# Twelve of sixteen expert-weight splits on GpSimd, all its down-weight work there too, and shorter lone recurrent steps in an adaLN, quantised-FFN, RNN and MoE kernel

## The reference

```python
def layer(x, cond, ...):
    # 1. per-batch modulated and normalised 128x128 weight times x   (L0_cond)
    # 2. quantised FFN; each act_qdq divides by the max |value| of a WHOLE tensor:
    x = act_qdq(x)
    up   = act_qdq(x @ lpbq_dequant(w_up).T)       # weights: one scale per 32 values
    gate = act_qdq(x @ lpbq_dequant(w_gate).T)
    gate = act_qdq(gate * fixed_qdq_u16(sigmoid(gate)))
    x1   = x_in + act_qdq(gate * up) @ lpbq_dequant(w_down).T
    # 3. recurrence over 128 times, 16 batches: h = tanh(x1_t @ Wx + b + h @ Wh)
    # 4. MoE: 8 experts of 512 hidden units, top 2 by router logits of h, softmax gates
    out  = x1 + sum_of_two(gate_e * (gelu(h @ w1_e.T + b1_e) @ w2_e.T + b2_e))
```

## Time and profile before

| what | value |
|---|---|
| runs | 293.18, 294.99, 294.94 us; median 294.94 |
| profiled execution | 293.55 us, of it span 291.8 us |
| PE / PEld busy | 259.8 / 204.2 us (89% / 70%) |
| DVE busy | 254.5 us (87%) |
| ACT busy | 213.6 us (73%) |
| POOL busy | 77.7 us (27%) |

### The profile page before, as it was taken

The page is one execution under the profiler, slowest core; times in us unless marked ns, Lnnn a source line. Parts: engine busy times, 40 slices in busy tenths (PEclk is TensorE's granted clock), DMA queues, the critical chain, the costliest instruction groups (busy, mean ns, idle before and its releaser), DMA issues.

```text
span 291.8 us, 7134 instructions
## 1 busy us (share of the span) xinstructions
PE 259.8 (89%) x2726; PEld 204.2 (70%) x2726; DVE 254.5 (87%) x629; ACT 213.6 (73%) x455; POOL 77.7 (27%) x148
## 2 busy tenths in 40 slices
PE   8999550068999999999999999999999999999994
PEld 4844240027856889888887888888778878878784
DVE  4997999999997899799887899788799987899875
ACT  5889899997832778677766766766567667688992
POOL 3368997050025412113112103111110411101000
PEclk9999955569999999999999999999999999999999
DMA  6993342103300000000000000000001000001000
GB/s 185 313 333 73 76 79 50 22 0 68 78 2 0 1 2 3 2 0 21 2 2 1 2 19 10 3 2 0 2 3 36 3 2 0 2 2 39 0 3 27
DMA packets 24039, 10.75 MB, mean 37 GB/s; under 512 B 13355, under 2 KB 22982, under 8 KB 24006
## 3 DMA queue, kind: packets, MB, share of 16 engines
q1 hardware_dynamic: 23470, 10.05, 13.9%
q10 hardware_dynamic: 536, 0.26, 0.3%
HBM read 6.11 MB, written 1.05 MB: 25 GB/s over the span
## 4 chain that ended last, share of the span: by engine, by line
PE 73%; DVE 10%; issue 1%; ACT 1%; DVEq 0%
PE bank L905 73%; DVE big L737 2%; DVE peak L645 2%; DVE big L884 1%; DVE big L749 1%; PE bank L1040 0%; DVE wyT L791 0%; DVE x_sb L771 0%; DVE big L880 0%; DVE big L756 0%; DVE big L744 0%; DVE c L764 0%; ACT wyT L465 0%; DVE wyT L839 0%; ACT big L552 0%
## 5 line engine op out<-in xcount | busy, mean ns | idle before, releaser
L905 PE MATMUL bank<-big,wt 128*128 128x384 f16 (+2 forms) x480 | 124.3, 336 | 0.5 <-DVE big L884 0.5
L905 PE MATMUL bank<-wt,big 128*128 128x128 f16 x1536 | 110.8, 219 | 0.5 <-DVE big L884 0.5
L905 PEld LDWEIGHTS bank<-wt,big 128*128 128x128 f16 x1536 | 98.2, 97 | 16.1 <-DVE big L884 0.7
L884 DVE TENSOR_TENSOR big<-big 128x384 f16<-128x384 f32 (+2 forms) x160 | 93.0, 587 | 18.1 <-ACT big L603 14.1
L601 ACT ACTIVATE big<-bank,miscT 128x384 f32<-128x384 f32 (+2 forms) x160 | 96.2, 602 | 13.6 <-PE bank L905 10.5
L905 PEld LDWEIGHTS bank<-q,wxh 128*128 128x128 f32 x254 | 44.9, 190 | 13.6 <-ACT q L564 2.0
L905 PEld LDWEIGHTS bank<-big,wt 128*128 128x128 f16 x480 | 49.6, 117 | 4.3 <-issue 0.6
L589 ACT ACTIVATE q<-bank 128x16 f32<-128x16 f32 x112 | 20.5, 183 | 38.0 <-PE bank L905 37.7
L414 POOL CAST big<-q 128x64 f16<-128x64 f32 x32 | 12.4, 388 | 125.7 <-ACT q L589 123.2
L880 DVE CAST big<-big 128x512 f16<-128x512 f32 (+2 forms) x104 | 39.0, 375 | 4.4 <-ACT big L601 4.2
L839 DVE SCALAR_TENSOR_TENSOR wyT<-bank,gates,wyT 128x128 f32<-128x128 f32 x128 | 39.8, 343 | 0.1
(11 more groups left out here) (168 smaller groups left out, 310.7 us busy)
## 6 DMA issues: line engine op xcount, KB each, us to landing
wnat<-in_w SPq DMA_DIRECT2D x8, 512.0 KB, 7.4
x_sb<-in_x SPq DMA_DIRECT2D x4, 256.0 KB, 4.4
out_block<-wyT SPq DMA_DIRECT2D x15, 64.0 KB
wn<-in_w_gate ACTq DMA_DIRECT2D x1, 192.0 KB, 4.8
wn<-in_w_up SPq DMA_DIRECT2D x1, 192.0 KB, 5.8
wn<-in_w_down SPq DMA_DIRECT2D x1, 192.0 KB, 5.8
b_in<-in_b SPq DMA_DIRECT2D x12, 4.0 KB
wt<-wyT SPq DMA_TRANSPOSE x8, 3.0
```

The costliest lines, as they stand in the source:

```text
L884: V.tensor_tensor(g_lo[:, par, f, 0:w], g32[:, f, 0:w], g_hi[:, par, f, 0:w], ALU.subtract).then_inc(g_lo_done, 1)
L905: return nc.tensor.matmul(o, l, r, start=start, stop=stop, skip_group_check=True)
```

## The change

- `W_POOL` goes from 8 to 12: chunks 8 to 11 are split on GpSimd, and SP transposes both parts. The buffer still has eight places (`NATS`), so GpSimd first waits for the eight earlier transposes. Four chunks are left to ScalarE and TensorE, and ScalarE's wait in front of them is now for twelve DMAs. `spread_peak(4)` stands before the last of them.
- `scale_weights(2)` goes ahead of the splits; the two parts of the down weights are made on GpSimd, behind chunk 11 and the parts of b2, from an fp32 copy that ScalarE takes out of PSUM (`wd32`, `wd_done`). The block scales of up and down are made in one set, in the front.
- `split_weights(0, 1)` goes ahead of `scale_weights(1)`.
- VectorE: `weight_lo(1)` one peak later; the first quarter of gate x sigmoid goes into the trip of peak 2; nothing is left in the trips of peaks 3 and 4.
- ScalarE: the two g2 quantisations go ahead of the Gelu table and of the four copies of x.
- The first 256 columns of the recurrence's input use one fp32 matmul on `x1` in place of three on its parts, so `split_x1(0)` goes; the first steps start half-way through chunk 1 in place of ahead of chunk 2. The transposes of x1 stand between the lone steps, the fourth group in the MoE's slot 1.
- The router's two parts are one operand of 16 columns; VectorE adds the halves as it copies them.
- The last expert's three tiles have a bank each, so each can be added when its own matmuls are done.
- `WARM_Q` goes from 8 to 2.

```diff
-W_POOL = 8
+W_POOL = 12
...
-WARM_START, WARM_COND, WARM_C, WARM_Q = 5, 2, 4, 8
+WARM_START, WARM_COND, WARM_C, WARM_Q = 5, 2, 4, 2
...
             scale_weights(0)
+            pool.wait_ge(c_mm, NK)
+            split_weights(0, 1)
             scale_weights(1)
...
-            pool.wait_ge(c_mm, NK)
-            split_weights(0, EARLY_SPLITS)
+            scale_weights(2)
+            split_weights(1, EARLY_SPLITS)
...
-            split_weights(EARLY_SPLITS, W_POOL)
-            scale_weights(2)
+            split_weights(EARLY_SPLITS, NATS)
+            split_b2()
+            pool.wait_ge(wt_t[0], 16 * NATS)
+            split_weights(NATS, W_POOL)
+
+            pool.wait_ge(wd_done, 1)
+            G.tensor_copy(wT_hi[:, 2 * NJ:NW, :], wd32[:, :, :]).then_inc(wT_hi_done, 1)
+            pool.wait_ge(wT_hi_done, 3)
+            G.tensor_tensor(wT_lo[:, 2 * NJ:NW, :], wd32[:, :, :], wT_hi[:, 2 * NJ:NW, :], ALU.subtract).then_inc(wT_done, 1)
...
-            take_weights(2)
+            act.wait_ge(wT_mm, 3)
+            A(wd32[:, :, :].rearrange("p j o -> p (j o)"), banks[W0_BANKS[2]][:, 0:NJ * P], ACT.Copy).then_inc(wd_done, 1)
             act.wait_ge(wt_t[0], 16 * W_POOL)
             weight_hi(W_POOL)
...
-            peak_to_scale(3, len(SIG_PARTS), lambda u: link(V.tensor_scalar(u, sc[:, 1, 2:3], 1.0 / 65536.0, None, ALU.mult)),
-                          lambda: block_peaks(2))
-            weight_scales(2)
+            for n in range(1, len(SIG_PARTS)):
+                gate_times_sigmoid(n)
+            peak_to_scale(3, len(SIG_PARTS), lambda u: link(V.tensor_scalar(u, sc[:, 1, 2:3], 1.0 / 65536.0, None, ALU.mult)))
...
             for i in range(W_POOL, W_CHUNKS):
-                if i == W_CHUNKS - 2:
+                if i == W_CHUNKS - 1:
                     spread_peak(4)
...
+            def first_input():
+
+                o = ps_rnn[:, 0:B * FIRST_STEPS]
+                mm(o, bh_rows[:, :], ones[:, 0:B * FIRST_STEPS], True)
+                mm(o, wxh[:, 0, :], x1[:, 0:B * FIRST_STEPS], False)
...
             for r in range(step, FIRST_STEPS):
                 first_step(r)
-            for k in range(NK):
+                if turned < NK - 1:
+                    transpose_x1(turned)
+                    turned += 1
+            for k in range(turned, NK - 1):
                 transpose_x1(k)
...
-                    mm(o, h_hi[:, t], rw_hi[:, :], j == 0)
-                    mm(o, h_hi[:, t], rw_lo[:, :], False)
-                    mm(o, h_lo[:, t], rw_hi[:, :], False)
-                    last = mm(o, h_lo[:, t], rw_lo[:, :], False)
+                    mm(o, h_hi[:, t], rw16[:, :], j == 0)
+                    last = mm(o, h_lo[:, t], rw16[:, :], False)
```

More of the change, by code:

```diff
@@ L57 @@
 LATE = NK - ACC_SCALAR
+TURN_AT = 1
 SIG_V = 1
@@ L673, in block_peaks, with weight_scales @@
                 link(V.tensor_reduce(ws[:, 0, 4 * NJ * n:4 * NJ * (n + 1)], wb, X, ALU.max, apply_absolute_value=True))
-            def weight_scales(n):
-                most, inverse, scale = (ws[:, i, 4 * NJ * n:4 * NJ * (n + 1)] for i in range(3))
+            def weight_scales(first, to):
+                most, inverse, scale = (ws[:, i, 4 * NJ * first:4 * NJ * to] for i in range(3))
                 link(V.tensor_scalar(most, most, 1.0 / 7.0, TINY, ALU.mult, ALU.max))
@@ L724, in round_sigmoid, with gate_times_sigmoid @@
                 V.tensor_scalar(part(sig2, SIG_PARTS[n]), part(sig2, SIG_PARTS[n]), SIG_MAX, SIG_MAGIC, ALU.min, ALU.add).then_inc(sig_round, 1)
[L726 to L735, removed]
+            def gate_times_sigmoid(n):
+                at = SIG_PARTS[n]
+                if n < SIG_V:
+                    round_sigmoid(n)
                 dve.wait_ge(*((sig_round, n + 1) if n < SIG_V else (sig_16, n - SIG_V + 1)))
@@ L739, in _ @@
                 block_peak(3, n, part(sig2, at))
-            peak_to_scale(3, len(SIG_PARTS), lambda u: link(V.tensor_scalar(u, sc[:, 1, 2:3], 1.0 / 65536.0, None, ALU.mult)),
-                          lambda: block_peaks(2))
-            weight_scales(2)
+            for i in (1, 2):
+                for k in range(i - 1, NK):
+                    peak_gate_up(i, k)
+                    if i == 1 and k == 1:
+                        weight_lo(1)
+                peak_to_scale(i, NK, lambda u: link(V.tensor_scalar(u, sc[:, 0, 2:3], 1.0 / WS, None, ALU.mult)),
+                              (lambda: peak_gate_up(2, 0)) if i == 1 else (lambda: gate_times_sigmoid(0)))
+            for n in range(1, len(SIG_PARTS)):
+                gate_times_sigmoid(n)
+            peak_to_scale(3, len(SIG_PARTS), lambda u: link(V.tensor_scalar(u, sc[:, 1, 2:3], 1.0 / 65536.0, None, ALU.mult)))
             link(V.tensor_scalar(part(sig2, P_PARTS[0]), part(sig2, P_PARTS[0]), sc[:, 3, 4:5], MAGIC, ALU.mult, ALU.add))
@@ L787, in _, with take_x1 @@
             split_x1(CH - 2)
-            dve.wait_ge(wt_t[1], 16 * (W_CHUNKS - W_POOL))
-            for k in range(ACC_SCALAR, NK):
+            split_x1(CH - 1)
+            def take_x1(k):
                 dve.wait_ge(x1T_mm, k + 1)
@@ L792, in _ @@
                               banks[ACC_BANKS[k]][:, :]).then_inc(added, 1)
-            split_x1(CH - 1)
+            dve.wait_ge(wt_t[1], 16 * (W_CHUNKS - W_POOL))
+            for k in range(ACC_SCALAR, NK - 1):
+                take_x1(k)
             dve.wait_ge(acc_s, ACC_SCALAR)
@@ L869, in pair @@
                         add_b2(c, 2)
+                    if c == 0 and first and s == TURN_AT + 1:
+                        take_x1(NK - 1)
                     if first and s == 2:
@@ L894, in _ @@
             dve.wait_ge(b2_added, CH)
[L895 to L899, removed]
+            dve.wait_ge(y_mm, CH * SLOTS - NF)
+            dve.wait_ge(added, LATE + E * TOK // P - 2 * TILES[-1])
+            for j in range(TILES[-1]):
+                add_gated(CH - 1, E - 2, j, ps_y[0])
+            for j in range(TILES[-1]):
+                dve.wait_ge(y_mm, CH * SLOTS + j)
+                dve.wait_ge(added, LATE + E * TOK // P - TILES[-1] + j)
+                add_gated(CH - 1, E - 1, j, LAST_Y[j])
         @block.tensor
@@ L1059, in _ @@
                     for j in range(NJ):
-                        if c >= 2 and (NJ * p + j) % STEP_EVERY == 1 and step < FIRST_STEPS:
+                        if (c >= 2 or (c == 1 and p >= 2)) and (NJ * p + j) % STEP_EVERY == 1 and step < FIRST_STEPS:
                             first_step(step)
@@ L1137, in pair @@
                         pe.wait_ge(acc_s, s - 1)
+                    if c == 0 and first and s == TURN_AT:
+                        transpose_x1(NK - 1)
                     if c == 0 and first and s == NF:
```

101 lines of the change are left out of this document (55 added, 46 removed).

## The result

| | before | after |
|---|---|---|
| all runs, median (lowest to highest) | 294.84 us (293.18 to 294.99), 7 runs | 296.35 us (295.56 to 296.93), 7 runs |
| profiled execution, its span | 293.55 us, 291.8 us | 296.93 us, 294.9 us |
| PE / DVE / ACT / POOL busy | 259.8 / 254.5 / 213.6 / 77.7 us | 253.8 / 255.6 / 209.7 / 96.9 us |

Ratio after to before 1.0064, 95% interval 1.0040 to 1.0088: slower by 1.9 us (1.2 to 2.6), by less than the 1% of the prediction's bound. TensorE has 6.0 us less to do, and the kernel is slower. Of the runs further down, one execution of e3 (1463.81 us) and one of e7 (319.77) lie far off the others; the medians count them, the ratios leave them out.

What follows compares the result with a forecast made beforehand. TensorE was taken to bound from 104.69 us on, VectorE from 38 to 76, TensorE then leading to the MoE. Terms 5.9 - 1.65 - 0.7 - 0.4 = +3.1 gave 298.0 on the median, lowered to 297.6; range 290 to 300.5.

Steps and rivals of the forecast that it cites:

- case 1: Whole kernel: the sum of the terms holds, T between 81.0 and 83.5, time 296 to 300 us; chance 0.62.
- T: Start of o's quantisation, 76.40 us before: predicted at 82.3, 5.9 later.
- GpSimd's schedule: GpSimd's twelve splits: 20.1 us of own work from 38.1, blocked 13.5 by VectorE's locking instructions, split 11 ending at 71.7.
- rival 2: Before T: split 11 slips in ahead of VectorE's last product, ends at 67.8, sum -0.9, 294 us; chance 0.13.
- Rival 3: Before T: GpSimd isn't held after 50 us, T is 74.2, sum -4.9, 290 us; chance 0.13.
- VectorE ready at about 73: VectorE before T: last peak at about 73, not 74.05, with 0.5 to 1.0 of waits for GpSimd.
- The clock: TensorE before T: 1.2 GHz at 75.7, first chunk 2.6 us, clock back at 78.5, 2.8 after matmuls begin.
- the landing: Split 11's transpose before T: lands 2.4 to 3.3 us later; 3.3 taken, giving 75.0.
- The front: Up to peak 2: split 0 early, gate and up peaks end within 0.6 of 37.8 as before.
- T to the MoE: From T to the MoE: MoE at T + 17.3, not T + 19.35; -1.65 at the point that was 104.69.
- Logits: MoE: 32 of 64 logit matmuls go, 28 under TensorE's bound; -0.7, range 0 to 0.8.
- End: Last additions: two of six run ahead of the last matmul, 0.6 less, but stores stay serial; -0.4.

Runs made afterwards that it cites:

- e3: Changed kernel with eight chunks split on GpSimd again and spread_peak(4) back at the last chunk but one; 293.55 us, ratio 0.9953 to the kernel before.
- e7: Changed kernel with ScalarE's tanh of step 0 ahead of its low byte of o's third chunk; 296.48 us, ratio 1.0068 to the kernel before.
- e1: Changed kernel with ScalarE's wait before its own four chunks set back to eight transposes; 294.32 us, ratio 1.000 to the kernel before.
- e2: Changed kernel with the splits of chunks 8 to 11 cut to 8 of 512 columns; 292.04 us, ratio 0.9907 to the kernel before.
- e4: Changed kernel with split 0 behind the up scaling again, twelve splits kept; 301.19 us, ratio 1.0227 to the kernel before.
- e6: Changed kernel with the edits of e1 and e4 together; 292.29 us, ratio 0.9924 to the kernel before.
- e8: Changed kernel with ten splits on GpSimd and the edits of e1, e4, e5 and e7; 291.35 us, ratio 0.9885 to the kernel before.
- e5: Changed kernel with one wait for the last three additions in place of three; 296.51 us, ratio 1.0059 to the kernel before.

## Why the prediction was right, and where its steps were not

The forecast was a sum of +3.1 us and 297.6; the runs give +1.9 and 296.35, inside the range and just inside case 1's own. The likeliest outcome by the chances, slower by over 1% (0.46), didn't come; 0.64% is within 1% (0.39). The sign and the mechanism (ScalarE's wait for twelve, a cold TensorE, peak 4's trip behind three chunks) are what e1 shows: with the wait cut to eight, the ratio goes from 1.0064 to 1.000. But that the two profiles differ by just +3.1 is luck: 0.61 of it is ahead of S, the trace before is of a short execution, and the terms' errors cancel. T is 1.11 less than the sum has it, the stretch to the MoE and the end 0.42 and 0.65 more.

**GpSimd's schedule: right in kind, too late in sum.** Split 11's end was put at 71.7 and came at 69.95, or, from S, 55.2 in place of 57.5. Splits 0 to 4 ended at 39.50 and not at 38.1: of the 1.4 that they are late 0.61 is S, and the up scaling had begun at 18.70 where I put 17.5. From there the own work was 20.35, near the 20.1 laid out, but the lock blocked 10.1 us and not 13.5. The term that failed is the 13.5. I let every locking instruction of VectorE start at its old time and hold GpSimd for its whole length. Where GpSimd was first, VectorE waited, and so came later: its last product went from 67.27 to 69.89, when split 11 was all but done, and held the down weights' cast, which had time. Its 3.2 are nearly all of the 3.4 that are missing. This slip is rival 2's event, which had a chance of 0.13; it put the end at 67.8, 53.6 from S, and the measured 55.2 lies between the two cases. That the time still fell into case 1's range is luck too. Rival 3, no lock after 50 us, is refuted by the steps of 1.67, 1.47, 1.59 and 2.66 us there.

**VectorE ready at about 73: wrong, the plainest error.** It was 76.67. The products and scalings from 38 us on were longer than alone by 3.7 us in sum (0.29, 0.10, 0.98, 0.52, 0.82 and 0.99), against 1.8 before; for the 1.9 more I had allowed "0.5 to 1.0". Another 0.69 was a wait for ScalarE's sigmoid behind peak 2: its copies out of PSUM ended at 35.98, 1.8 later than before (34.19), behind up transposes that were 2.2 later (22.78 for 20.58), and my sum had no such term. And 0.75 of the savings was booked at the wrong place: the `weight_lo` of the down weights stood behind the last peak (74.68 before), so leaving it out could bring T forward but not that peak. The block peaks and down scales did save 0.98. It didn't show in the end only because peak 4's trip was later still. e1 took that cover off: its T is 1.08 later than before, from S, and not earlier. e2 shows that the four extra splits make the delay, and e4 that it hangs on how the two streams meet.

**The clock: direction right, return too early.** TensorE was at 1.2 GHz at 73.72, the first chunk took 2.62 (2.6 predicted), and 2.4 GHz came back at 78.0, 4.3 us after it started, not 2.8. So peak 4's transpose stood 6.13 behind the first chunk's start and not 5.35: +0.8. In sum, from S: 2.4 less for the split, 0.2 less for the landing (3.1 in place of 3.3), 0.8 more for the clock: T +4.2 in place of +5.9.

**The front.** Split 0's early place was to cost nothing that shows ("within 0.6 of 37.8"). Peak 2 came at 38.73, of that 0.61 is S; the step on q beside split 0 took 1.52 and not 0.69. From S to peak 2 it is 23.96, before 23.65; with split 0 early it is 23.69 to 24.27 in the six traces, and 23.04 or 23.05 with split 0 put back (e4, e6, e8). The idle 3.67 us of GpSimd were free for GpSimd alone.

**T to the MoE: -1.65 predicted, -1.23 measured.** The fp32 input cost 0.54 (0.5 predicted), one lone step was left, as said. The MoE's first input came at T + 17.98 (99.17), where 17.3 was predicted. The shortfall is at the steps inside chunk 1: TensorE waited 0.78 for a tanh, where 0.3 was allowed. My first reading, the low byte's place, was too simple: e7 moved it and nothing was gained. ScalarE has 1.48 us of work to fit between steps that are 0.7 apart, and in both places tried a step waits for it.

**Logits: right.** -0.69 against -0.7. The second chunk's logits after (TensorE's timeline):

```profile
126.78 0.29 PE L932 MATMUL bank<-rw,big 128*128 128x16 f16 x6
126.93 0.49 PE L932 MATMUL bank<-big,wt 128*128 128x384 f16 x2
```

They start within 0.15 us, where twelve needed 0.31: 16 columns cost no more than 8.

**End: sign wrong.** -0.4 predicted, +0.25 measured, from 3.8 us behind the last matmul to 4.05. No addition of the last expert ran ahead, since VectorE was still with the expert before; the separate waits then put the last three 0.45 apart (290.89, 291.34, 291.80). By the traces of e5 and e8 one wait gives the 0.3 back.

The sum of the measured terms is 4.79 - 1.23 - 0.69 + 0.25 = 3.12, the difference of the spans (3.1).

## What to carry to other kernels

When work goes to an idle GpSimd, count it twice: what VectorE's multiplies hold up there, and what it holds up on VectorE, which may be the chain that leads. Lay both streams out together and move each instruction as the other delays it; a schedule of one against the fixed times of the other got the long instructions at the end wrong here, and there one place more or less was worth 3 us. And a wait should name the buffers it needs: with the wait for eight the changed kernel is even with the one before (1.000), with the wait for twelve it loses (1.0064), and another edit's sign came out the other way. In combination, ten splits with the short wait and split 0 in its old place gained 1.15% (e8).

## What the runs showed of the hardware beyond what I expected

- The lock between VectorE and GpSimd works in VectorE's direction too. A product that meets a GpSimd step of 1.15 us that has just begun is longer by nearly that (64.25: 3.28 for 2.29). The Trainium skill, page "SBUF — State Buffer", section "Who interferes with whom", says that whoever issues first has the ports for the whole instruction and the other blocks fully; the trace agrees, now on both sides and between 50 and 74 us as well. In the prediction I used that rule for GpSimd's delays and hardly for VectorE's. I also gave the section's exception for instructions with one SBUF input without its condition, that they are outside the 2-port modes: VectorE's scaling of 59.67 has one SBUF input and took 1.20 beside GpSimd, 0.68 before.
- What the lock costs isn't smooth. A GpSimd step of 0.51 to 0.62 us took 3.71 and 3.80 under the longest product. Where it was a cast with time to spare nothing came of it; where it was a step of split 10 (e4) T moved by 5.0 us.
- Pauses of TensorE of 1.43 and 1.70 us with one chunk between them were followed by 1.2 GHz from 76.0 to 79.3 us (e6), in the middle of the down projection, and chunk 1 began 0.85 later behind T; with a pause of 1.10 ahead of the down projection (e8) the clock stayed at 2.4 GHz. In e1 a pause of 3.14 was followed by 1.2 GHz from 76.2 to 79.6, and chunk 1 began 2.98 behind T all the same.
